# Two layers of cross attention on one core: four groups of four heads with stages between them, or one pipeline over eight groups of two heads

## What is computed

```python
xn = layernorm(ctx); ln = layernorm(latents)        # 6404 and 1024 rows
q  = ln @ Wq                                        # 16 heads of 64
kv = concat([xn @ Wkv, ln @ Wkv])                   # 7428 keys
qn = rmsnorm(q, qn_g) * scale;  kn = rmsnorm(k, kn_g)
sim = where(mask, einsum('bhid,bhjd->bhij', qn, kn), max_neg)
out = einsum('bhij,bhjd->bhid', softmax(sim), v) @ Wout + bout
```

## Time and profile before

| | us |
|---|---|
| median of 3 runs | 4764.76 (4763.67 to 4764.98) |
| profiled execution | 4763.29 |
| its span, first to last instruction | 4761.5 |
| PE, DVE, ACT busy | 4319.0, 3613.2, 3270.6 |
| a group of layer 0: steady part, boundary | 501, 86 |
| a group of layer 1: steady part, boundary | 433.7, 76.1 |
| mean granted TensorE clock | 0.946 of 2.4 GHz |

### The profile page before, as it was taken

How to read it: one execution, slowest core, us unless ns; L and a number is a source line. 1 busy time by engine, 2 the same in 40 slices (tenths; PEclk the granted TensorE clock), 3 DMA queues, 4 the chain that set the end, 5 groups by cost and what they waited for, 6 DMA issues and landing times. The chain is left out here.

```text
span 4761.5 us, 76929 instructions
## 1 busy us (share of the span) xinstructions
PE 4319.0 (91%) x25711; PEld 2658.2 (56%) x25711; DVE 3613.2 (76%) x5350; ACT 3270.6 (69%) x5554; POOL 506.0 (11%) x443
## 2 busy tenths in 40 slices
PE   2899979999699996999987699979998999979996
PEld 1566645666456664666655366646665566646654
DVE  6788868888688885888843588858886788768875
ACT  2899948999389993999922477737774677557770
POOL 2111111111111111111100100000000000000000
PEclk8899989999899997999988799989999999989997
DMA  2000000000000000000001000000000000000000
GB/s 51 1 0 0 0 3 1 0 0 0 3 0 0 0 0 1 0 0 0 0 36 47 3 0 0 1 2 0 0 0 2 0 0 0 2 0 0 0 0 9
DMA packets 15431, 19.45 MB, mean 4 GB/s; under 512 B 2704, under 2 KB 11256, under 8 KB 15096
## 3 DMA queue, kind: packets, MB, share of 16 engines
q1 hardware_dynamic: 9204, 14.52, 1.0%
q10 hardware_dynamic: 6148, 3.89, 0.3%
HBM read 17.87 MB, written 0.52 MB: 4 GB/s over the span
## 5 line engine op out<-in xcount | busy, mean ns | idle before, releaser
L647 DVE TENSOR_TENSOR a_probs_lo<-a_probs 128x1024 fp32r<-128x1024 f32 x1760 | 2112.3, 1222 | 580.4 <-ACT a_probs L562 322.0
L558 ACT ACTIVATE a_probs<-scores_ps,a_c_neg,a_k_rstd 128x512 f32<-128x512 f32 x1888 | 1315.1, 778 | 187.4 <-PE scores_ps L829 187.4
L562 ACT ACTIVATE a_probs<-scores_ps,a_c_neg 128x1024 f32<-128x1024 f32 x816 | 865.2, 1112 | 446.3 <-PE scores_ps L829 446.2
L854 PE MATMUL out_ps<-a_probs_lo,a_v 128*128 128x512 f32 x3520 | 1052.7, 420 | 0.0
L847 PE MATMUL out_ps<-a_probs,a_v 128*128 128x512 bf16 x3520 | 947.4, 388 | 12.0 <-DVE a_out_acc L660 12.0
L829 PE MATMUL scores_ps<-a_q_hi,a_k_hi 64*128 64x512 f32 x3520 | 795.1, 446 | 6.2 <-DVE a_k_lo L765 5.9
L854 PEld LDWEIGHTS out_ps<-a_probs_lo,a_v 128*128 128x128 f32 x3520 | 661.1, 188 | 186.6
L829 PE MATMUL scores_ps<-a_q_lo,a_k_hi 64*128 64x512 f32 x3520 | 706.6, 393 | 0.0
L829 PE MATMUL scores_ps<-a_q_hi,a_k_lo 64*128 64x512 f32 x3520 | 703.8, 393 | 0.0
L660 DVE TENSOR_TENSOR a_out_acc<-out_ps,a_out_acc 128x512 f32<-128x512 f32 x896 | 575.0, 683 | 58.9 <-PE out_ps L854 36.1
L847 PEld LDWEIGHTS out_ps<-a_probs,a_v 128*128 128x128 f16 x3520 | 302.6, 97 | 455.8 <-issue 202.5
(11 more groups left out here) (196 smaller groups left out, 3696.6 us busy)
## 6 DMA issues: line engine op xcount, KB each, us to landing
squares<-in_L_xattn_Wkv SPq DMA_DIRECT2D x16, 128.0 KB, 2.3
m_w<-in_L_ffn_w1T SPq DMA_DIRECT2D x1, 2048.0 KB, 7.7
m_w<-in_L_ffn_w2T SPq DMA_DIRECT2D x1, 2048.0 KB, 12.1
a_w_q<-in_L_xattn_Wq ACTq DMA_DIRECT2D x2, 512.0 KB
normed_T<-in_L_xattn_Wout SPq DMA_DIRECT2D x64, 0.5 KB
a_w_e<-in_L_xattn_Wo SPq DMA_DIRECT2D x64, 0.5 KB
residual<-in_x SPq DMA_DIRECT2D x1, 512.0 KB, 3.8
a_w_o<-in_L_xattn_Wout ACTq DMA_DIRECT2D x1, 512.0 KB
```

The source lines that it names most:

```text
L558: ins = nc.scalar.activation(probs[:, n % NB, e * 512:(e + 1) * 512], scores[:, n % 2, e * 512:(e + 1) * 512], ACT.Exp, bias=cneg[:, p:p + ...
L562: ins = nc.scalar.activation(probs[:, n % NB, :], scores[:, n % 2, :], ACT.Exp, bias=cneg[:, p:p + 1])
L647: nc.vector.tensor_tensor(plow[:, n % NPL, :], probs[:, n % NB, :], p_hi[:, n % NB], ALU.subtract).then_inc(plo_ready, 1)
L854: nc.tensor.matmul(outs[:, e * 512:(e + 1) * 512], v32[:, par, 2 * p + e, t, :], plow[:, n_ % NPL, e * 512:(e + 1) * 512], start=False, st ...
```

## The change

- Groups have two heads, and there are eight. A unit is one chunk against one half of the queries; chunks have 4 to 6 tiles by a table. An item is two tiles for two heads: six matmuls of 256 columns.
- The loop over groups is the only loop. Its body is a whole group, written out; scores of the next group's first steps stand in the last pair of this one. `schedule` places the item transposes ("turn") and projections ("load") in the pairs at slots s, m or e (start, middle, end), and picks free pairs for the output projection of the group before (`FINAL`) and the query projection and transposes of the next (`Q_ROW`, `Q_COL`). All of these use the one bank `proj`.
- The output projection works on transposed output, 512 queries at a time, with high and low parts. The denominators go through DRAM to be spread over partitions. `oacc` is written by a copy at first, so nothing clears it.
- The mask is a bias of the exponential (0 or -10000) together with the bound. Values are read with a fixed scale; their low part is taken from PSUM, so the key transpose waits for DVE too.
- `x_hi`, `x_lo` are made once, in the preparation, for all tiles. Weights come from arrays laid out by group on the host.

```diff
-GH = 4
+GH = 2
-CT = 4
-NB = 8
+CHUNKS = ((6,) * 9 + (5,), (6, 6, 6, 6, 6, 4, 4, 4, 4, 5))
+NB = 6
+def schedule(L):
+    ...
+    steps = [(c, n, t) for c, m in enumerate(tiles) for n in range(2) for t in range(m)]
+    slots = (("s", 0.2), ("m", 0.55), ("e", 1.0))
+    for c, pairs in enumerate(tiles):
+        n_items = (tiles[(c + 1) % len(tiles)] + 1) // 2
+        for k in range(2 * n_items):
+            at = (k + 1) * pairs / (2 * n_items)
+            _, pair, slot = min((abs(p + x - at), p, s) for p in range(pairs) for s, x in slots)
+            where = turn if k % 2 == 0 else load
+            where[first[c] + pair] = (slot, item0[c + 1] + (k + 1) // 2)
+    ...
+    free = [p for p in sorted(load) if load[p][0] == "e" and turn.get(p - 1, " ")[0] == "e" and p - 1 not in ends]
+    final = [p for p in free if p >= 5][:4]
+    q_row = [p for p in free if p > final[-1]][:2]
+    q_col = [p for p in free if p >= q_row[1] + 6][:2]
 preparation, layer 0, ACT and POOL, per job of four tiles
-                                ins = nc.scalar.activation(dst, src, ACT.Identity, bias=col[:, 1:2], scale=col[:, 0:1])
+                            nc.scalar.activation(xt[:, i % 2, 0:w], src, ACT.Identity, ...)
+                            nc.scalar.activation(hi, xt[:, i % 2, 0:w], ACT.Copy).then_inc(xh_done, 1)
+                            nc.gpsimd.tensor_tensor(lo, xt[:, i % 2, 0:w], hi.bitcast(F32), ALU.subtract).then_inc(xl_done, 1)
 preparation, layer 1, DVE, per job
+                                ins = nc.vector.tensor_tensor(lo, src, hi.bitcast(F32), ALU.subtract)
 ACT
-                    nc.scalar.activation(vrow, proj[:, GH * DH:2 * GH * DH]..., ACT.Copy, scale=m)
+                    nc.scalar.activation(v16[:, par, 2 * j:2 * j + 2, :, 0:DH]..., proj[:, 2 * P:4 * P]..., ACT.Copy, scale=1.0 / LIFT)
-                def v_hi(g, c, j, par):
-                def key_ones(c, par):
-                def x_high(c, par):
+                for i in range(NPR):
+                        if i == NPR - 1:
+                            act.wait_ge(p_ready, s0 + NS)
+                            bias_set(g + 1)
+                        for k in range(2):
+                            exp(s0, k0, 2 * i + 2 + k)
+                        if i == 0:
+                            e_high(g)
+                        if i < GH:
+                            o_high(g, i)
+                        if i == 2:
+                            wo_split(g)
+                        ...
+                        if i in Q_ROW:
+                            q_rows(g + 1, Q_ROW.index(i))
+                        ...
+                        for kind, k in EVENTS.get(i, []):
+                            if kind == "turn":
+                                k_high(k0, k)
+                                v_wide(k0, k)
+                            else:
+                                ...
+                                read_kv(k0, k)
 DVE
+                    for i in range(NPR):
+                        p_low(s0, 2 * i + 2)
+                        if i in FINAL:
+                            final_mul(g, f, side_no(g, "final", f))
+                        ...
+                        p_low(s0, 2 * i + 3)
+                        if i in ENDS and not crossed:
+                            add_out(g, s0, *ENDS[i][0])
+                        if i in FINAL:
+                            final_add(...)
+                        if i < GH:
+                            o_low(g, i)
+                        if i == 2:
+                            wo_low(g)
+                        if i in (3, 4):
+                            den_inv(g, i - 3)
+                def p_low(s0, n2):
+                    if n2 >= NS:
+                        dve.wait_ge(mixed, 2 * (s0 + n2) - 2)
 SP
+                def load_den(r):
+                    sp.wait_ge(o_added, 2 + r * NADD)
+                    sp.dma_start(den_row.unsqueeze(0), oacc[P - 1:P, :, :]).then_inc(den_out, 16)
+                    sp.wait_ge(den_out, 16 * (r + 1))
+                    sp.wait_ge(c_ready, r + 1)
+                    sp.dma_start(den[:, :, :], den_row.partition_broadcast(P)).then_inc(den_in, 16)
 PE
-                    for n, (x, w) in enumerate(((x_h, w_h), (x_h, w_l), (x_l, w_h))):
-                        last = nc.tensor.matmul(proj[:, :], x[:, par, j * P:(j + 1) * P], w[:, :], start=n == 0, stop=n == 2)
+                    pe.wait_ge(side_read, sides)
+                    for t in range(2):
+                        for m, (a, w) in enumerate(((x_hi, wkv_h), (x_hi, wkv_l), (x_lo, wkv_h))):
+                            last = nc.tensor.matmul(dst, a[:, x], w[:, :]..., start=t == 0 and m == 0, stop=m == 2, ...)
+                def project_q(r, b, freed):
+                    for j in range(4):
+                        for m, (a, w) in enumerate(((l_hi, wq_h), (l_hi, wq_l), (l_lo, wq_h))):
+                            last = nc.tensor.matmul(proj[:, j * P:(j + 1) * P], a[:, q], w[:, :], ...)
+                def final(r, f, freed):
+                    nc.tensor.matmul(proj[:, :], wo_h[:, w], o_hi[:, e, q], start=True, stop=False)
+                    nc.tensor.matmul(proj[:, :], wo_l[:, w], o_hi[:, e, q], start=False, stop=False)
+                    nc.tensor.matmul(proj[:, :], wo_h[:, w], o_lo[:, e, q], start=False, stop=False)
+                    nc.tensor.matmul(proj[:, :], we_h[:, f * D:(f + 1) * D], e_hi[:, :], start=False, stop=True)
-                    project_q(g * (GH * DH) + GH * DH)
-                    pe.wait_ge(o_added, (g + 1) * (2 * NUNIT) + 2 * ONE)
-                    for t in range(QT):
-                            nc.tensor.matmul(fin_bank(t, h % 2)[:, at:at + D + 1], oacc[:, h, t * P:(t + 1) * P], ...)
+                    for i in range(NPR):
+                        for k in range(2):
+                            score(s0, k0, g, 2 * i + 2 + k)
+                        ...
+                        pe.wait_ge(p_ready, s0 + 2 * i + 2)
+                        if i % 2 == 1 or i == NPR - 1:
+                            ... mix_last(n1)
+                        item(i, "s")
+                        if i in FINAL:
+                            final(g, FINAL.index(i), k0 + TURN[i - 1][1] + 1)
+                        if i in Q_ROW:
+                            project_q(g + 1, Q_ROW.index(i), ...)
+                        if i in Q_COL:
+                            transpose_q(g + 1, Q_COL.index(i), ...)
+                        mix_high(g, 2 * i)
+                        mix_high(g, 2 * i + 1)
+                        item(i, "m")
+                        mix_low(s0, 2 * i)
+                        mix_low(s0, 2 * i + 1)
+                        item(i, "e")
```

More of the change, by code:

```diff
@@ L444, in attention_layer, with tile_par, place @@
+        def tile_par(c):
+            return c % 2
+        def place(k):
+            k = k % NI
+            c = max(c for c in range(NCH) if ITEM0[c] <= k)
+            return c % 2, k - ITEM0[c]
+        T_LAST = TL[NCH - 1] - 1
         with nc.Block() as block:
@@ L818, in transpose_k @@
+                def transpose_k(k0, k):
+                    pe.wait_ge(kv_read, k0 + k + 1)
+                    pe.wait_ge(v16_done, k0 + k + 1)
+                    for t in range(2):
+                        last = nc.tensor.transpose(proj[:, t * P:(t + 1) * P],
+                                                   krow[:, 2 * t:2 * t + 2, :].rearrange("p h d -> p (h d)"), ident[:, :])
                     last.then_inc(kt_done, 1)
-                def score(b, u, t, par, item=None, freed=None):
-                    p, n = u // 2, u % 2
+                def project_q(r, b, freed):
+                    pe.wait_ge(wq_lo, r + 1)
@@ L842, in mix_high, with mix_last @@
-                def mix_high(n_, u, t, par, unit):
-                    p = u // 2
-                    for e in range(2):
+                def mix_last(n1):
+                    c, n, t, idx = step_at(n1)
+                    for e in range(GH):
+                        j = 32 * (2 * e + n1 % 2)
+                        last = nc.tensor.matmul(last_ps[j:j + 32, :], vlast[:, c % 2, t, e, 4 - 4 * n:36 - 4 * n],
+                                                p_hi[:, idx % NB, e * 512:(e + 1) * 512],
+                                                start=n1 < 2, stop=True, skip_group_check=True)
+                    return last
@@ L982, in _ @@
                 if L == 1:
-                    rstd(pool, QT, var2, rstd2, 1)
+                    rstd(pool, QT, var_ready, rstd_ready, 3)
+            @block.tensor
+            def _(pe):
+                pe.wait_ge(lat_ready, 2)
+                for t in range(QT):
+                    last = nc.tensor.transpose(scores[:, t // 4, (t % 4) * P:(t % 4 + 1) * P], YT[:, t * P:(t + 1) * P], ident[:, :])
+                last.then_inc(tr_done, 1)
             @block.vector
             def _(dve):
-                step = Steps(dve, end_step)
```

(17 more changed lines are left out.)

1239 lines of the change are left out of this document (685 added, 554 removed).

## The result

The changed kernel takes 4993.6 us (median of 4 runs, 4993.29 to 4994.86) against 4764.2 us before: ratio 1.048, 95% interval 1.047 to 1.049. It is 229 us slower; the forecast was 4520 us, 244 us faster.

A forecast was written before the change was run, and what follows sets the result against it. TensorE was taken to bound the kernel. Preparation, heads, groups (2134 and 1862 us), tails, the stretch between layers and the end summed to 4521, rounded to 4520 us; range 4450 to 4590, or 4440 to 4640 with deeper stalls.

The forecast's parts named there:

- The bound and the removed boundaries: Whole kernel: TensorE sets the steady pace; six boundaries, 486 us, go, and their TensorE work moves inside the pipeline.
- price list: TensorE costs from the earlier timeline: bare pair 3.52 us, last-dimension matmuls 0.57 per two pairs, transposes 0.27, key projection 0.69.
- Items: Key and value projections: six 256-column matmuls take 0.69 us, an item 0.96 with transposes; total as before.
- The rival that they would not pay: Narrow key projection: weight loads make each item cost 0.69 us more, +309, 4829 us in all; chance 0.06.
- The query projection: TensorE side work per group: 24 matmuls of 128 columns at 0.17 us each, 4.1 us.
- ACT and DVE: Layer 0 groups: both engines reach 86% and neither passes TensorE, so their added side work costs nothing on average.
- rival of deeper stalls: Seams and side work: stalls of 10 us per group rather than 4, +96, 4616 us; chance 0.17.
- Seam: Handover at each group end: 4 us taken, between 0 and about 8.
- ring: Seam part: with four low-part places, the first step waits until an old-group step is mixed; 2 us.
- jump: Seam part: the outer loop's jump back stalls for an instruction fetch; 3 us, from a 3.05 us idle row.
- Heads, tails, preparation: Outside the groups: heads 42 and 35 us, tails 26 each, preparation 6 us longer in layer 0 and 21 in layer 1.

The follow-up runs named there:

- the experiment with columns: Changed kernel with the sums inverted in full as 128 x 16 through DRAM, and the output weights' loads moved ahead of the broadcast: 4748.1 us.
- the last kernel: Four mends together with two groups written out per loop turn, plus the key item's early low halves ahead of the two output additions on the vector engine: 4529.6 us.
- Four mends together: Changed kernel with the reciprocal by columns, the bias three pairs later, a fifth place for low halves and the key weights' split one item earlier: 4612.6 us.

## Why the prediction was wrong

*The bound and the removed boundaries*: right. TensorE sets the pace of ordinary pairs, the six boundaries are gone, and a pair with the last-dimension matmuls and nothing else is 4.09 as in the price list (pair 27 of layer 1).

*Items*: right. Six matmuls of 256 columns start 0.12 us apart (full clock), 0.72 for the 0.69 taken. The rival that they would not pay is refuted. The query projection was cheaper than taken: its pairs are 6.19 for 4.79, 1.40 for 12 matmuls, 0.117 each for 0.17.

*ACT and DVE*: **this step failed**, by the size of one term and by what the step takes it to mean. It reads "two reciprocals, four multiply and four add of 512 columns, by 1.22 and 0.68 us", sums the side work to 17 us, DVE to 86% of a group, and ends "Neither passes PE, so these cost nothing on average". The reciprocals take 6.54 us each and not 1.22: 13.1 us a group, not 2.4. I priced an operation that the trace of before shows only in small shapes by the row of another kind. Even the right average would not have helped: at 6.54 us the DVE is still under TensorE's pace over the groups (busy 77% of them in layer 0 and 75% in layer 1), and it cost 13 to 15 us a group all the same, since TensorE needs a low half in every pair and DVE gives none for 6.54 us, twice within three pairs. By the experiment with columns this is 245 of the 470 us, the tails' share included. (The sum has a slip too: 218 - 13 + 17 is 222 and not 225, which changes nothing.) A price was there to be had, for the trace of before holds two shapes of reciprocal:

```profile
L779 DVE RECIPROCAL a_fin_rec<-proj_ps 128x2 f32<-128x2 f32 x32 | 5.4, 170 | 52.2 <-PE spare_ps L973 52.2
L779 DVE RECIPROCAL a_fin_rec<-spare_ps 128x2 f32<-128x2 f32 x32 | 4.8, 150 | 0.0
L1091 DVE RECIPROCAL m_gate<-m_gate 128x8 f32<-128x8 f32 x2 | 0.4, 202 | 0.1
```

From 2 to 8 columns it grows by 32 to 52 ns, 5.3 to 8.7 ns a column, so an estimate for 1024 columns is 5.6 to 9.0 us, and 6.54 lies in it. (It is rough: the 2-column ones read PSUM and the 8-column one SBUF.)

The Trainium skill, "VectorE: DVE Perf Modes", section "First, the fixed hardware budget", says that the reciprocal is an iterated division with a repeat count of 8. The traces agree in kind: 6.25 ns a column, 5.2 times the 1.2 of a subtraction. The section gives no time, but it is reason enough to doubt the 1.22 us.

*Moved waits*: not in the forecast at all. I asked what is queued behind ACT's bias copy, and not what is queued behind DVE's wait for the bound (L859), nor behind the split of the next key weights. Both stand ahead of the low halves on DVE and, since a key's transposes now wait for the value's low half, TensorE stops. Moving them gave 60 and 62 us. The prediction's rival of deeper stalls had the right kind ("every key transpose now waits for DVE too") and the wrong size: it allowed 6 us a group over the 4 and would have needed 30.

*Seam*: 4 us taken, bounds 0 to 8. It is 9.4 us in layer 0 (11.80 + 6.16 less 4.8 and 3.74), outside the bounds: the failure is one of size and of two links left out. The parts I named, ring and jump, are real (2.2 and 3.6 us by their experiments). Two were missing: the additions ahead of the key's low half (52 us in all of its places), and that the stops bring the clock down, so that the matmuls behind take nearly twice as long (L1025's start 0.21 us apart for 0.12). The jump was named with a row, and then taken inside a mean of 4; its 3.05 us there and 3.6 to 3.9 us here agree.

The Trainium skill, "Runtime: NRT & Kernel Launch", section "Instruction fetch mechanics", which the prediction cites, puts such a stall down to a fetch of the jump's target. The traces agree in kind: half as many jumps save 29 to 31 us, and the queue of instruction transfers on the profile's page carries 4.15 MB in the changed kernel, 3.88 with half the jumps and 0.79 before. Code twice as long showed no cost besides.

*Heads, tails, preparation*: within 15 us each. The first query matmul comes at 91.6 us for 92. Heads are 27 and 29 for 42 and 35; but in layer 0 15 us then pass from the first score to the second pair, where TensorE waits 6.1 us for the first exponentials. Tails are 33 and 32 for 26; the reciprocals, 13 us for the 2.4 taken, are more than the whole difference (in the last kernel, with the reciprocal by columns, layer 0's tail is 22 us).

What the price list was worth can be read from the last kernel: with the five stalls mended and half the jumps gone it has 271.4 and 232.6 us a group (forecast 266.7 and 232.8) and 4529.6 us in all (forecast 4520). The estimate of the work was near, that of the order was not. That the whole comes within 10 us is in part luck, though: layer 0's groups take 44 us more than forecast (2178 for 2134 us), and the heads, the tails and the rest some 38 us less.

Two things stay open. Four mends together bring 22 us less than one by one; the pair times show where they overlap (pairs 54, 29 and 0 of layer 0, 46 and 0 of layer 1, each shortened by more than one of the mends) but not why. And layer 0's groups are still 4.7 us each over the forecast.

## What to carry to other kernels

Price each new instruction by its own kind and its own number of columns; where the trace has only small ones of that kind, take the slope from two of them and not from another kind, and move the work to a shape of few columns if it matters. An engine's mean free time says little of what an added instruction costs: for each instruction put into a steady loop, and each wait, ask what stands behind it in the same queue and whether the bounding engine takes it in the same pair. And when several pipelines are made one, list the pair times of one period and look for the odd ones: four places here held nearly all the loss, and a few lines moved or changed mended each.

## What the hardware showed unexpectedly

- RECIPROCAL on the vector engine: 0.15 to 0.17 us for 2 columns, 0.19 for 8, 0.246 for 16, 1.74 for 256, 6.54 for 1024 (fp32, 128 partitions).
- PARTITION_ALL_REDUCE of two columns on GpSimd is listed with 0.37 us in the lines above, and the instruction that waits for it starts 7.19 us after it began (7.05 to 8.56 in the changed kernel).
- The jump back at the end of a turn whose body is a whole group costs 3.6 to 3.9 us, and it shows as "issue" in front of the first score.
